# Layer statistics, row extremes and weight quantisation of a quantised feed-forward moved into the attention ahead of it

## The reference

```
x = x + _L1_xattn_ref(_layernorm(x), ctx, Wq, Wk, Wv, Wo, bo)
x = x + _L1_ffn_ref(_layernorm(x), W1, b1, W2, b2)

def _affine_quantize(x):
    amin, amax = (jnp.min(x), jnp.max(x))                 # over all of x
    scale = jnp.maximum((amax - amin) / 255.0, 1e-08)
    zp = jnp.clip(jnp.round(-amin / scale) + QMIN, QMIN, QMAX)
    q = jnp.clip(jnp.round(x / scale) + zp, QMIN, QMAX)
def _sym_quantize(w):
    scale = jnp.maximum(jnp.max(jnp.abs(w)) / 127.0, 1e-08)
    q = jnp.clip(jnp.round(w / scale), -127.0, 127.0)
def _qlinear(x, W, b):
    acc = einsum(xq - zx, wq); return acc * (sx * sw) + b
h = gelu(_qlinear(x, W1, b1)); out = _qlinear(h, W2, b2)
```

## Time and profile before

| | |
|---|---|
| median of 3 runs | 2571.04 us (2566.32 to 2573.92) |
| the profiled execution: its time, its span | 2571.09 us, 2569.3 us |
| mean granted TensorE clock | 0.939 of full speed |
| busy share of the span | PE 89%, PEld 77%, DVE 73%, ACT 57%, POOL 20% |
| second attention: first instruction, first and last residual | 807.50, 842.27, 1135.40 us |
| QuantFfn: first instruction, first shift of x by ACT | 1135.77, 1188.90 us |
| second range (third PARTITION_ALL_REDUCE) | 1284.32 us |

### The profile page before, as it was taken

One profiled execution on the slowest core, in us unless ns is written; L12 is line 12 of the kernel. 1 busy time (PEld: TensorE's weight loads), 2 busy tenths in 40 slices (PEclk: granted clock), 3 DMA queues, 4 the chain that ended last, 5 costly groups with the idle time before them and its releaser, 6 DMA issues.

```text
span 2569.3 us, 49258 instructions
## 1 busy us (share of the span) xinstructions
PE 2287.2 (89%) x14961; PEld 1969.9 (77%) x14962; DVE 1869.3 (73%) x4436; ACT 1459.9 (57%) x2849; POOL 513.8 (20%) x700
## 2 busy tenths in 40 slices
PE   7899999999798999952458999999996998979997
PEld 6788888888597888841146888888885787879997
DVE  3778878778754888877873778888886665756665
ACT  5455565555344566624776666666663563646665
POOL 2022222222101121101001111111112341412333
PEclk9999999999899999985658999999998999989999
DMA  8444454444101444420013554545541000024444
GB/s 207 114 132 123 121 147 125 131 139 125 54 0 51 123 131 136 138 61 1 0 34 101 148 146 137 147 139 139 139 125 45 1 1 14 27 61 132 131 131 136
DMA packets 460456, 256.53 MB, mean 100 GB/s; under 512 B 25440, under 2 KB 441468, under 8 KB 460348
## 3 DMA queue, kind: packets, MB, share of 16 engines
q1 hardware_dynamic: 460348, 255.27, 35.9%
HBM read 150.10 MB, written 105.12 MB: 99 GB/s over the span
## 4 chain that ended last, share of the span: by engine, by line
PE 71%; DVE 13%; ACT 6%; issue 6%; POOL 1%; DVEq 1%; DMA 1%; ACTq 0%; SPq 0%; POOLq 0%
PE ps_o L780 11%; PE ps_s L764 11%; PE ps_p L87 6%; PE ps_p L88 6%; PE ps_p L89 6%; PE ps_t L753 6%; PE ps_o L1216 3%; PE ps_t L1216 2%; DVE a_sm L1007 2%; DVE a_e L1015 2%; DVE a_mx L996 2%; PE ps_s L87 2%; PE ps_t L2767 2%; PE ps_o L2767 1%; PE ps_s L89 1%
## 5 line engine op out<-in xcount | busy, mean ns | idle before, releaser
L780 PEld LDWEIGHTS ps_o<-a_val,a_pt 128*128 128x128 f32 (+2 forms) x3200 | 414.7, 193 | 35.0 <-issue 9.2
L764 PE MATMUL ps_s<-a_keys,a_zt 128*128 128x308 f32 (+1 forms) x1024 | 419.3, 494 | 14.5 <-ACT a_keys L879 6.8
L780 PE MATMUL ps_o<-a_val,a_pt 128*128 128x128 f32 (+2 forms) x3200 | 425.5, 276 | 6.7 <-ACT a_pt L916 3.9
L1007 DVE TENSOR_REDUCE a_sm<-a_e 128x16 f32<-128x1232 f32 (+1 forms) x192 | 234.3, 1220 | 226.7 <-ACT a_e L924 224.8
L888 ACT ACTIVATE a_stage<-ps_p 128x512 f32<-128x512 f32 (+1 forms) x370 | 221.1, 598 | 290.9 <-PE ps_p L89 289.8
L916 ACT ACTIVATE a_pt<-ps_t 128x512 f32<-128x512 f32 (+1 forms) x448 | 225.4, 505 | 161.7 <-PE ps_t L753 161.3
L879 ACT ACTIVATE a_keys<-ps_p 128x308 f32<-128x308 f32 x603 | 257.4, 427 | 102.5 <-PE ps_p L89 102.3
L996 DVE TENSOR_REDUCE a_mx<-ps_s 128x6 f32<-128x462 f32 (+1 forms) x512 | 255.5, 548 | 62.1 <-PE ps_s L764 41.1
L753 PE MATMUL ps_t<-ident,a_e 128*128 128x128 f32 (+1 forms) x1600 | 262.2, 276 | 31.6 <-DVE a_e L1015 29.2
L87 PE MATMUL ps_p<-ct_hi,a_mt_hi 96*128 (+1 forms) x603 | 258.9, 429 | 0.0
L1015 DVE TENSOR_TENSOR a_e<-a_e,a_rs 128x1232 f32<-128x1232 f32 (+1 forms) x192 | 251.7, 1311 | 6.6
(11 more groups left out here) (392 smaller groups left out, 4675.3 us busy)
## 6 DMA issues: line engine op xcount, KB each, us to landing
a_vals<-a_stage SPq DMA_DIRECT2D x160, 512.0 KB, 3.5
a_val<-a_vals SPq DMA_DIRECT2D x128, 576.0 KB
f_w<-in_L_ffn_W_dram SPq DMA_DIRECT2D x129, 256.0 KB, 2.6
a_vals<-a_stage SPq DMA_DIRECT2D x40, 416.0 KB
a_val<-a_vals SPq DMA_DIRECT2D x64, 256.0 KB
a_val<-a_vals SPq DMA_DIRECT2D x128, 40.0 KB
x<-in_x_dram SPq DMA_DIRECT2D x8, 512.0 KB, 7.6
out_dram<-x SPq DMA_DIRECT2D x8, 512.0 KB, 5.4
```

Of the source, the lines that this page charges most:

```text
L764: mm = eng.matmul(o, zt, keys[:, h0:h0 + nh, :], start=True, stop=not self.masked)
L780: mm = eng.matmul(c.ps_o[:, (i % 2) * P:(i % 2 + 1) * P], self.pt[0:r, n, :], self.val[0:r, i % 2, n, :], start=(n == 0), stop=(n == self. ...
L1007: eng.tensor_reduce(self.sm[:, :], e, AX.X, ALU.add).then_inc(st.sem, 1)
```

## The change

A new class `TailRanges` takes the statistics and extremes of the rows over from QuantFfn and spreads them over the second attention:

- ACT: at the end of each tile t of the attention, one Copy activation over tile t - 1 with scale -1/128 whose accumulated sum is the negated mean (tiles 0 to 59), and one Square activation over tile t - 4 with the negated mean as bias, whose accumulated sum gives the squares. Both write their 128x128 result to a place that nobody reads.
- DVE: `extremes` at k == 2 and k == 3 of every group but the last: maximum and minimum over two tiles of the group. In the last group `vector` does bn_stats, maximum, minimum and bn_aggr for one tile at a time, one tile behind the residual; the last two of them come behind the last residual.
- POOL: `root` per group, three groups behind: multiply by 1/128, add eps, power -0.5; the last four behind the last bias.
- The weights of QuantFfn are loaded by SP right behind the bias of the attention, and quantised by DVE (`quantise_weights`) ahead of the first `shift`; POOL reduces their maxima over the partitions ahead of its wait for the projections and of `copy_window(1)`.
- QuantFfn then begins with `normalised_range` and two small reductions. Its four statistics parts, its eight reductions over x, its roots and its weight steps are gone; the rows for ACT take two instructions in place of three.
- The first window of ACT's and of POOL's loop is written out ahead of the loop.

```diff
+class TailRanges:
+
+
+
+    SUMMED = BATCH - GT
+
+    def __init__(self, core, added, place):
+        self.core, self.added = core, added
...
+    def scalar(self, eng, t):
+
+        known = isinstance(t, int)
+        if not known or 1 <= t <= self.SUMMED:
+            eng.wait_ge(self.added.sem, self.added.at(t))
+            eng.wait_ge(self.summed.sem, self.summed.at(t - 1))
+            eng.activation(self.unread[0], self.tile(t - 1), ACT.Copy, scale=-1.0 / P,
+                           accum_out=self.neg_mean[:, ds(t - 1, 1)]).then_inc(self.summed.sem, 1)
+        if not known or t >= GT:
+            eng.wait_ge(self.summed.sem, self.summed.at(t - GT + 1))
+            eng.wait_ge(self.squared.sem, self.squared.at(t - GT))
+            eng.activation(self.unread[1], self.tile(t - GT), ACT.Square, bias=self.neg_mean[:, ds(t - GT, 1)],
+                           accum_out=self.squares[:, ds(t - GT, 1)]).then_inc(self.squared.sem, 1)
+
+    def extremes(self, eng, g, half):
+
+        b = GT * g + 2 * half
+        eng.wait_ge(self.added.sem, self.added.at(b + 2))
+        for m, op in enumerate((ALU.max, ALU.min)):
+            eng.tensor_reduce(self.x_range[:, m, ds(b, 2)], self.core.x[:, ds(b, 2), :], AX.X, op)\
+               .then_inc(self.ranged.sem, 1)
+
+    def root(self, eng, g):
+        c, cols = self.core, ds(GT * g, GT)
+        last = isinstance(g, int) and g == GROUPS - 1
+        eng.wait_ge(self.root_step.sem, self.root_step.at(3 * g + 1))
+        if last:
+            eng.wait_ge(self.last_aggr.sem, self.last_aggr.at(GT))
+            eng.tensor_tensor(self.var, self.mv[:, :, 1], c.eps[:, :], ALU.add).then_inc(self.root_step.sem, 1)
+        else:
+            eng.wait_ge(self.squared.sem, self.squared.at(GT * g + GT))
+            eng.tensor_tensor(self.var, self.squares[:, cols], self.per[:, :], ALU.mult)\
+               .then_inc(self.root_step.sem, 1)
+            eng.wait_ge(self.root_step.sem, self.root_step.at(3 * g + 2))
+            eng.tensor_tensor(self.var, self.var, c.eps[:, :], ALU.add).then_inc(self.root_step.sem, 1)
+        eng.wait_ge(self.root_step.sem, self.root_step.at(3 * g + 2 + (0 if last else 1)))
+        eng.tensor_tensor(self.rstd[:, cols], self.var, c.neg_half[:, :], ALU.pow).then_inc(self.root_step.sem, 1)
+
+    def gpsimd(self, eng):
+        eng.memset(self.per[:, :], 1.0 / P).then_inc(self.root_step.sem, 1)
+
+    def vector(self, eng, t):
+
+        k = t % GT
+        eng.wait_ge(self.added.sem, self.added.at(t + 1))
+        eng.bn_stats(self.stats[:, k, :], self.tile(t)).then_inc(self.last_stats.sem, 1)
+        for s, op in enumerate((ALU.max, ALU.min)):
+            eng.tensor_reduce(self.x_range[:, s, t:t + 1], self.tile(t), AX.X, op).then_inc(self.last_range.sem, 1)
+        eng.wait_ge(self.last_stats.sem, self.last_stats.at(k + 1))
+        eng.bn_aggr(self.mv[:, k, :], self.stats[:, k, :]).then_inc(self.last_aggr.sem, 1)
+
+    def normalised_range(self, eng, do):
+
+        eng.wait_ge(self.last_aggr.sem, self.last_aggr.at(GT))
+        do(eng.tensor_scalar(self.neg_mean[:, self.SUMMED:BATCH], self.mv[:, :, 0], -1.0, None, ALU.mult))
+        eng.wait_ge(self.summed.sem, self.summed.at(self.SUMMED))
+        eng.wait_ge(self.ranged.sem, self.ranged.at(4 * (GROUPS - 1)))
+        eng.wait_ge(self.last_range.sem, self.last_range.at(2 * GT))
+        both = lambda a: a.unsqueeze(1).broadcast_to([P, 2, BATCH])
+        do(eng.tensor_tensor(self.x_range, self.x_range, both(self.neg_mean), ALU.add))
+        eng.wait_ge(self.root_step.sem, self.root_step.at(3 * GROUPS))
+        do(eng.tensor_tensor(self.x_range, self.x_range, both(self.rstd), ALU.mult))
+        do(eng.tensor_tensor(self.scaled_mean, self.neg_mean, self.rstd, ALU.mult))
@@ -671,6 +766,8 @@
             self.after.load(eng)
+        if self.left:
+            self.quant.load(eng)
         for u in range(self.units):
@@ -975,8 +1072,14 @@
                 copy_next(self.WIN)
-
-        with eng.Fori(0, self.WINDOWS - 1) as w:
+                if self.left:
+                    self.left.scalar(eng, t)
+
+        first = 0
+        if self.left:
+            window(0, False)
+            first = 1
+        with eng.Fori(first, self.WINDOWS - 1) as w:
             window(w, False)
@@ -1055,6 +1158,8 @@
         self.ln.vector_stats(eng, 1)
+        if self.left:
+            self.quant.quantise_weights(eng)
         self.shift(eng, 0, 0)
@@ -1078,6 +1183,10 @@
                     self.next_stats.tile(eng, t - 1)
+                if self.left and last and k > 0:
+                    self.left.vector(eng, t - 1)
+                elif self.left and not last and k >= 2:
+                    self.left.extremes(eng, g, k - 2)
                 if self.next_stats and self.setup and last:
@@ -1089,6 +1198,8 @@
             self.next_stats.tile(eng, BATCH - 1)
+        if self.left:
+            self.left.vector(eng, BATCH - 1)
         eng.sem_inc(self.done.sem, 1)
@@ -1100,6 +1211,9 @@
         self.ln.pool_bias(eng, 0)
+        if self.left:
+            self.left.gpsimd(eng)
+            self.quant.over_partitions(eng, 0)
         eng.wait_ge(self.proj_done.sem, self.proj_done.at(self.vuses))
@@ -1112,6 +1226,8 @@
                     self.next_stats.pool(eng, g - 2)
+                if self.left and not (isinstance(g, int) and g < 3):
+                    self.left.root(eng, g - 3)
             if more:
@@ -1120,7 +1236,11 @@
         else:
-            with eng.Fori(0, self.WINDOWS - 2) as w:
+            first = 0
+            if self.left:
+                groups(0, True)
+                first = 1
+            with eng.Fori(first, self.WINDOWS - 2) as w:
                 groups(w, True)
@@ -1128,6 +1248,9 @@
                 self.next_stats.pool(eng, g)
+        if self.left:
+            for g in range(GROUPS - 4, GROUPS):
+                self.left.root(eng, g)
 
@@ -1544,46 +1661,34 @@
 
-    def sync(self, eng):
+    def load(self, eng):
+
         s, sem = self.src, self.loaded.sem
-        eng.wait_ge(self.before.sem, self.before.at(1))
         with self.core.nc.allow_non_contiguous_dma("small columns"):
...
             eng.dma_start(self.b1[:, :], s["b1"].rearrange("(c p) -> p c", p=P)).then_inc(sem, 16)
+
+    def sync(self, eng):
+        s = self.src
+        eng.wait_ge(self.before.sem, self.before.at(1))
         eng.wait_ge(self.bias_clear.sem, self.bias_clear.at(2))
...
 
+    def over_partitions(self, eng, n):
+        eng.wait_ge(self.reduce_ready.sem, self.reduce_ready.at(n + 1))
+        eng.partition_all_reduce(self.all[:, n, :], self.red[:, n, :], P,
+                                 bass.bass_isa.ReduceOp.max).then_inc(self.reduced.sem, 1)
+
     def gpsimd(self, eng):
-        c = self.core
         eng.wait_ge(self.before.sem, self.before.at(1))
-
-        def over_partitions(n):
-            eng.wait_ge(self.reduce_ready.sem, self.reduce_ready.at(n + 1))
-            eng.partition_all_reduce(self.all[:, n, :], self.red[:, n, :], P,
-                                     bass.bass_isa.ReduceOp.max).then_inc(self.reduced.sem, 1)
-
-        def invert(q):
-            part = slice(self.TILES * q, self.TILES * (q + 1))
-            eng.wait_ge(self.aggr_ready.sem, self.aggr_ready.at(self.TILES * (q + 1)))
-            eng.tensor_tensor(self.var[:, part], self.mv[:, part, 1],
-                              c.eps[:, 0:1].broadcast_to([P, self.TILES]), ALU.add).then_inc(self.rstd_step.sem, 1)
-            eng.wait_ge(self.rstd_step.sem, self.rstd_step.at(2 * q + 1))
-            eng.tensor_tensor(self.rstd[:, part], self.var[:, part],
-                              c.neg_half[:, 0:1].broadcast_to([P, self.TILES]), ALU.pow).then_inc(self.rstd_step.sem, 1)
-
         eng.memset(self.ones[:, :], 1.0).then_inc(self.bias_clear.sem, 1)
-        invert(0)
-        over_partitions(0)
-        for q in range(1, self.PARTS):
-            invert(q)
-        over_partitions(1)
+        self.over_partitions(eng, 1)
 
...
         eng.memset(self.bias[:, :], 0.0).then_inc(self.bias_clear.sem, 1)
-        over_partitions(2)
-
+        self.over_partitions(eng, 2)
 
@@ -1607,27 +1712,14 @@
 
-    def vector(self, eng):
-        c, C, T = self.core, self.C, self.TILES
+    def quantise_weights(self, eng):
+
         do = lambda ins: self.chain.step(eng, ins)
-        tile = lambda t, b: t[:, ds(b, 1), :].rearrange("p a d -> p (a d)")
-
-        def statistics(q):
-            with eng.Fori(T // GT * q, T // GT * (q + 1)) as g:
-                for k in range(GT):
-                    eng.bn_stats(tile(self.stats, GT * g + k), tile(c.x, GT * g + k)).then_inc(self.stats_ready.sem, 1)
-            eng.wait_ge(self.stats_ready.sem, self.stats_ready.at(T * (q + 1)))
-            for b in range(T * q, T * (q + 1)):
-                eng.bn_aggr(self.mv[:, b, :], self.stats[:, b, :]).then_inc(self.aggr_ready.sem, 1)
-
-        eng.wait_ge(self.before.sem, self.before.at(1))
-        statistics(0)
```

(41 more changed lines are left out.)

39 lines of the change are left out of this document (27 added, 12 removed).

## The result

The changed kernel takes 2537.8 us (median of 4 runs, 2534.6 to 2540.4) against 2571.3 (4 runs, 2566.3 to 2573.9): a ratio of 0.987, 95% interval 0.9856 to 0.9884, 33.5 us less. Forecast were 2547 (2532 to 2561) and faster. Its profiled execution took 2534.6 (span 2532.8), the lowest of the four.

What follows compares the result with a forecast made beforehand. QuantFfn's head was taken as bound by DVE alone, the attention by PE in step with the others. 2571.1 - 41.1 (head) + 16.8 (attention) = 2546.8, so 2547 us, range 2532 to 2561.

Steps and rivals of the forecast that it cites:

- The head: Start of QuantFfn, last residual to first shift of x: about 12 us left, a gain of 41.1 us.
- The windows: Seven windows of the second attention: added DVE and ACT work costs 2.36 us each, 16.5 us in all.
- The three places: Tiles i = 4, 5 and 0 of a window, where delays of 0.62, 0.82 and 0.92 us reach PE.
- A = 0.82: ACT's time in us for a tile's Copy and Square pair; bounds 0.4 and 1.4.
- 0.17 for k == 2: DVE's lateness in us from the extremes at k == 2; with 0.75 at k == 3, 0.92 reaches i = 0.
- The last window: Last window of the second attention: DVE's gap takes most of the pairs, cost 0.3 us.
- The weights at nothing: Attention's beginning: quantising the weights ends by 826.4, 3 us before DVE's first row maximum, and costs nothing.
- the way back: POOL after the weights' all-reduce: 7.07 us to return to tensor operations, so `copy_window(1)` ends at 832.3; no cost.
- POOL's roots at nothing: Attention windows: three small POOL operations a group, 1.5 us, behind `pool_bias`, cost nothing.
- Table loads: Rival: Square needs another table than Exp, two loads a tile for 60 tiles, 98 us more, 2645; chance 0.05.
- Dear sums: Rival: ACT's sums take 1.4 us or more a tile, delaying exponentials in five of eight places; 2555 to 2567, chance 0.22.
- Swallowed: Rival: the windows' spare DVE and ACT time absorbs the added work; 2530, or 2525 with cheap all-reduce; chance 0.12.

Runs made afterwards that it cites:

- dve_none: Changed kernel without DVE's extremes of groups 0 to 14 and without their wait and two semaphore increments; 2536.4 us.
- act_out: Changed kernel without ACT's Copy and Square sums per tile, their waits and increments kept, constants in their columns; 2534.9 us.
- deferred: Changed kernel with the extremes of a group's tiles 2 and 3 moved from k == 3 to k == 1 of the next group; 2537.9 us.
- act_early: Changed kernel with ACT's two sums ahead of the last value copy, in tiles whose copies end with a value copy; 2534.6 us.
- both_none: Changed kernel without ACT's sums and DVE's extremes of groups 0 to 14, nor their waits and increments; POOL's three operations stay; 2531.5 us.
- dve_out: Changed kernel without DVE's extremes of groups 0 to 14, their wait and two semaphore increments kept, a constant in their columns; 2540.1 us.
- weights_late: Changed kernel with the weights' maxima, all-reduce and quantisation moved back from the attention's beginning to the head of QuantFfn; 2543.2 us.

## Why the prediction was right, and where it was off

- **The head** (gain 41.1, measured 41.2). Every step of it held within 0.5 us. Counted from the start of the last residual, the power ended at 3.07 us (forecast 3.5), the memset at 3.2 (3.7), then came the gap of 5.88 (5.57) and PARTITION_ALL_REDUCE at 9.1 (9.3), the first shift at 12.3 (12.4). That the gap belongs to POOL's way from its earlier work to this instruction, and not to the instruction's start-up, is now shown by two kernels and not only read from two rows; that it is code being changed is still my name for it. The Trainium skill (GPSIMD Engine Reference, section Instruction dispatch) gives a load of about 6 us for the first call to a freshly loaded kernel, with no instruction of its own in the profile. The 5.88 us agree; that the time is paid again at a later change (824.06 and 1153.33 in the same execution) only the rows show.
- **The windows** (16.5, measured 8.9): the term that was mis-sized, 2.36 us a window against 1.26. The three places were the right ones, and A = 0.82 was right as well: the pair is Copy 0.30, Square 0.39 and two reads of 0.19, within 0.8. The step that failed is the one from an engine's added time to the delay at PE and at the residual; three subtractions were missed. The exponentials begin 0.50 us behind the start of the copy ahead of them (0.49 before the change), before its end; with the pair between they begin at 1.17, so it delays them by 0.67, not 0.82. DVE's pair of 0.74 takes the place of the 0.30 of issue that stood ahead of the row sum anyway and overlaps its neighbours, which leaves 0.36 where 0.92 was forecast (of the 0.17 for k == 2 nothing arrives). And the delays at i = 4 and 5 do not add: ACT's alone is worth 0.36 there (dve_none), DVE's alone 0.20 (act_out), both together 0.36. Even with 0.67 for the pair ACT's two places would come to 0.47 and 0.67, and they gave 0.36 and 0.53; where the other 0.11 and 0.14 went no run shows. The error was to add delays of an engine as delays of the end.
- **The last window** (+0.3, measured -1.3). This is TensorE's granted clock. In the kernel before it stood at 0.50, the level of 1.2 GHz, from 1130 to 1132; in the changed one at 1.00, 2.4 GHz, up to the last residual; in deferred again at 0.50. Windows of the changed kernel, then of deferred, columns as in the earlier trace rows:

```profile
1138.00:1140.00 2.00, 0.00 (x0) 0.00 (x0) 2.00 (x8) 1.27 (x4) 0.00 (x0) 1.00 0.53 158
1141.00:1143.00 2.00, 1.33 (x10) 0.95 (x10) 1.31 (x6) 0.90 (x3) 0.00 (x0) 1.00 0.00 0
```

```profile
1136.00:1138.00 2.00, 0.39 (x3) 0.42 (x4) 2.00 (x9) 1.74 (x5) 0.00 (x0) 1.00 0.49 145
1138.00:1140.00 2.00, 1.91 (x11) 1.61 (x10) 1.93 (x6) 0.01 (x1) 0.00 (x0) 0.57 0.00 0
1140.00:1142.00 2.00, 1.43 (x7) 1.04 (x6) 0.45 (x3) 1.15 (x4) 0.01 (x1) 0.50 0.00 0
```

  In deferred PE had been busy 0.39 of 2 us before the clock fell; in the changed kernel it was not busy at all from 1138 to 1140, and the clock did not fall. Over the thirteen kernels the last window is 27.3 us long in the four in which the clock stays at 1.00 (changed, act_out, act_early, both_none) and 28.5 to 29.5 in the nine in which it falls, in no order by what was changed. What decides it stays open. Among the four, the changed kernel (27.34) and both_none (27.31), which has neither the sums nor the extremes of the groups before, differ by 0.03 us: of the 0.3 forecast for the work added there nothing is seen.
- **The weights at nothing**: right, though the working was lucky. DVE finished at 829.2 where 826.4 was forecast. PARTITION_ALL_REDUCE started 2.0 us later than forecast (1.5 of them the later attention), and the quantisation took 4.7 us and not 3.8; 1.1 of that is one step that ran beside POOL's first copy (last section). POOL went on with `copy_window` at once, not after 7.07 us; the way back was paid behind it, where nobody waits.
- **POOL's roots at nothing**: right, by both_none. **Table loads**: none, that rival is gone. **Dear sums**: gone. **Swallowed**: nearer than I put it; the windows' real cost of 8.9 lies halfway.
- The sum was made for one execution: 2546.8 against the profiled 2534.6. Of these 12.2 us 7.6 are the windows' term, 1.6 the last window's, 0.4 the beginning and the head, and 2.6 lie in the stretches that the change doesn't touch (-4.1 and +1.5). Against the median the forecast is 9.0 high, about what the windows and the last window make together (9.2); but only one of the four runs has a profile, so how long the last window was in the others isn't known.

## What to carry to other kernels

A delay of one engine costs only what is left after the waits it runs into; where two engines are late in the same step, the larger one counts, so price a step by its latest wait and not by a sum. Work that fills an engine's gap belongs ahead of the instruction that waits for another engine, not behind it: the sums cost 0.6 us a window behind the last copy and nothing ahead of it. Put an operation that makes GpSimd change its code directly behind its last tensor operation, ahead of anything that waits, so that the change runs while the engine would idle: here the order alone took the head from 10.5 to 6.9 us.

## What the runs showed of the hardware

- The gap ahead of PARTITION_ALL_REDUCE (5.57 to 6.36 us in all rows of the thirteen kernels in which it isn't hidden) runs once that instruction is next in GpSimd's queue, though its own semaphore is not there yet; a wait of 16.98 us ahead of a memset before it hid none of it. A CAST (824.32) or MEMSET (1149.55) behind it starts at once; a TENSOR_TENSOR needs another 6.97 us, even with two CASTs between (833.87), and 6.7 to 7.6 in the other kernels with early weights.
- A sum read out by ACT is an instruction of its own: 0.19 to 0.22 us each.
- A wait and two semaphore increments with no work between cost DVE 0.28 us (issue 0.58 in place of 0.30; period 38.94 in dve_out, 38.65 in dve_none).
- DVE's step over 128x2 elements took 1.23 us beside POOL's first CAST (from 824.47) and 0.17 without one (1154.47 of weights_late). It ends at 825.70, the CAST at 825.66, though the two work on different tiles. In both_none it is the same (1.28 us, CAST first by 0.06 us), and in the nine kernels in which DVE's step began before the CAST it took 0.17. The Trainium skill (SBUF — State Buffer, section Who interferes with whom) says that VectorE in one of its two-port modes and GpSimd share a pair of ports, and that the later one waits for the whole instruction of the other; the rows agree, though none shows in which mode the step runs.
